# Three attentions computed with transposed scores in PSUM

## The reference

```python
x = x + tanh(g_xattn[n]) * attention_n(layernorm(x), ctx, ctx)
x = x + tanh(g_ffn[n]) * ffn_n(layernorm(x))
```

## Time and profile before

| | us |
|---|---|
| median of 3 runs | 3622.13 (3612.05 to 3623.86) |
| profiled execution | 3616.34 |
| its span | 3614.6 |
| PE / DVE / ACT / POOL busy | 2554.5 / 2132.0 / 1498.5 / 1596.1 |

### The profile page before, as it was taken

The page is one execution under the profiler, slowest core; times in us unless marked ns, Lnnn a source line. Parts: engine busy times, 40 slices in busy tenths (PEclk is TensorE's granted clock), DMA queues, the critical chain, the costliest instruction groups (busy, mean ns, idle before and its releaser), DMA issues. The chain is left out here.

```text
span 3614.6 us, 84054 instructions
## 1 busy us (share of the span) xinstructions
PE 2554.5 (71%) x30961; PEld 1981.4 (55%) x30971; DVE 2132.0 (59%) x4394; ACT 1498.5 (41%) x2492; POOL 1596.1 (44%) x2184
## 2 busy tenths in 40 slices
PE   5999999977678886233687766609956877665490
PEld 4878778764557775122465555506634665554260
DVE  3767777661166664676578788854424666677312
ACT  3555555532255553677343333202215665553120
POOL 1333433440164430775024666440017788884207
PEclk9999999988888887555688778659976766675795
DMA  4000000003300000000000000015531000000243
GB/s 143 17 18 22 23 21 21 20 8 112 99 26 22 22 19 13 1 1 1 26 10 12 23 22 23 20 61 153 161 106 32 23 25 27 27 23 13 79 128 93
DMA packets 192979, 153.50 MB, mean 42 GB/s; under 512 B 24426, under 2 KB 170461, under 8 KB 192582
## 3 DMA queue, kind: packets, MB, share of 16 engines
q1 hardware_dynamic: 176198, 116.45, 11.0%
q0 software_dynamic: 16384, 31.69, 2.9%
HBM read 97.54 MB, written 52.43 MB: 41 GB/s over the span
## 5 line engine op out<-in xcount | busy, mean ns | idle before, releaser
L979 PE MATMUL l_B<-l_val,l_prob_t 128*64 128x18 f32 x6144 | 348.6, 220 | 44.1 <-ACT l_prob_t L822 36.9
L979 PEld LDWEIGHTS l_B<-l_val,l_prob_t 128*64 128x64 f32 x6144 | 340.4, 149 | 59.3 <-issue 59.3
L903 PE MATMUL l_PT<-const_table,l_prob 128*128 128x128 f32 x1536 | 267.9, 332 | 38.0 <-ACT l_prob_t L822 28.6
L1971 PE MATMUL experts_H<-experts_xs_t,experts_w 128*128 128x512 f32 x576 | 272.1, 616 | 10.1 <-ACT experts_hid L1951 4.9
L903 PEld LDWEIGHTS l_PT<-const_table,l_prob 128*128 128x128 f32 x1536 | 237.3, 178 | 68.8 <-issue 58.0
L822 ACT COPY l_prob_t<-l_PT 128x512 f32<-128x512 f32 x384 | 209.6, 601 | 132.8 <-PE l_PT L903 132.7
L203 POOL DMA_INDIRECT l_got<-rows,l_index x192 | 220.2, 1147 | 94.7 <-POOL l_index L196 50.3
L358 POOL TENSOR_TENSOR l_products<-l_router_w,xn_all 128x1024 f32<-128x1024 f32 x100 | 236.3, 2390 | 32.3 <-DVE logits L464 32.0
L883 PE MATMUL l_A<-const_table,l_xn 128*128 128x128 f32 x192 | 59.6, 410 | 251.7 <-issue 139.1
L328 POOL DMA_INDIRECT slots<-xn_all,put x192 | 202.0, 1052 | 60.6 <-issue 49.5
L632 POOL TENSOR_TENSOR l_var_eps<-l_mv,eps 128x2 f32<-128x2 f32 x96 | 26.4, 275 | 430.4 <-DVE l_mv L775 430.3
(11 more groups left out here) (309 smaller groups left out, 6835.8 us busy)
## 6 DMA issues: line engine op xcount, KB each, us to landing
experts_w<-in_F_w SPq DMA_DIRECT2D x104, 256.0 KB, 2.9
experts_xs<-slots SPq DMA_DIRECT2D x72, 256.0 KB, 2.8
rows<-experts_y SPq DMA_DIRECT2D x72, 256.0 KB, 2.9
l_ctx_t<-in_ctx_t SPq DMA_DIRECT2D x96, 128.0 KB, 2.1
slots<-l_zeros SPq DMA_DIRECT2D x64, 96.0 KB
experts_w<-in_F_w SPq DMA_DIRECT2D x40, 128.0 KB, 2.5
slots<-l_zeros SPq DMA_DIRECT2D x8, 512.0 KB, 5.5
l_ctx_t<-in_ctx_t SPq DMA_DIRECT2D x64, 64.0 KB, 2.0
```

Of the source, the lines that this page charges most:

```text
L903: last = nc.tensor.transpose(PT[:, c % 2, P * a:P * a + P], prob[:, t.par(5), c, a // 2, 2 * (a % 2):2 * (a % 2) + 2, :].rearrange("p j k ...
L979: last = nc.tensor.matmul(B[64 * b:64 * b + 64, col:col + 18], prob_t[:, 4 * (hp // 2) + 2 * tile + hp % 2, 64 * b:64 * b + 64], val[:, t. ...
L1971: nc.tensor.matmul(H[:, c, :], w1_s[:, t.par(2), c, :], xs_t[:, t.par(2), :], start=True, stop=True).then_inc(h_filled[c], 1)
```

## The change

`attention_narrow` becomes `attention_split`, `Tail` becomes the `Router` that the wide attention already had (now shared). In L1 and L2 the scores are made twice: S as before, query rows by key columns, only to find each row's maximum; and P, key rows by query columns, in PSUM banks Z, from which the row maximum is subtracted by matmuls (the maximum is split in bf16 parts, turned by TensorE, spread on a diagonal by VectorE, and multiplied by minus ones). ScalarE takes Exp of P straight from PSUM, and the result is already the form in which TensorE multiplies it with the values, one head at a time with a column of ones for the sum. In L3 there is no maximum, and P alone is made; relu and Ln/Exp parts are kept apart and added by TensorE's accumulation. Heads are numbered so that the rows of the four heads of a group alternate row by row; the masked copies of q and k are made by four DMAs each with a row step of four into cleared buffers. In L1 and L2 one free stage lies between projection (4) and S (6), P is stage 7, values 8, stream 9; in L3 P is stage 6, values 7, stream 8. The biases of v and o enter by bf16 matmuls of three rows. `Head` loses its index copies, and gathers behind the combination of the item before.

```diff
         if t.live(out):
...
-        if t.live(s + 2) and not self.on_dve(t, s + 2):
-            pool.wait_ge(self.w_in, self.loads)
-            wait(pool, self.xn_done, n2)
-            wait(pool, self.summed, n3)
-            for tile in range(k):
-                last = nc.gpsimd.tensor_tensor(self.prod[:, tile, :, :], self.w_s[:, :, :],
-                                               g.xn[:, bass.ds(t.item(s + 2) * k + tile, 1), :].broadcast_to([P, EXPERTS, D]),
-                                               ALU.mult)
-            last.then_inc(self.multiplied, 1)
...
-            V.tensor_reduce(g.logits[:, bass.ds(t.item(s + 3) * k, k), :], self.prod[:, :, :, :], AX.X, ALU.add).then_inc(self.summed, 1)
...
+            last = nc.tensor.matmul(out[:, EXPERTS * tile:EXPERTS * tile + EXPERTS], self.xn_t[:, t.par(s + 3), tile, :], self.w_s[:, :],
+                                    start=True, stop=True)
...
-def attention_narrow(nc, g, name, gate_col, wq, bq, wk, bk, wv, bv, wo, bo, kind, mask=None, head=None, tail=None):
+def attention_split(nc, g, name, gate_col, wq, bq, wk, bk, wv, bv, wo, bo, kind, mask=None, head=None, router=None):
...
+    STAT, NORM, TURN, PROJ = 1, 2, 3, 4
+    SCORE, PROB, OUT, STREAM = (5, 6, 7, 8) if stable else (6, 7, 8, 9)
+    SLOTS_QK, SLOTS_CTX = 4, 8
+    LAST = STREAM + 1
...
+        QK = X[:, 0, :] if stable else Z[:, 0, :]
+        XV = Z[:, 1, :]
+        TOP, WO, TURNED, RANKS = X[:, 0, 0:P], X[:, 1, 0:256], X[:, 2, :], X[:, 3, :]
...
+                    slot, before = t.par(PROJ, SLOTS_QK), PROJ + SLOTS_QK
+                    if not stable:
+                        wait(sp, qk_drained, t.done(PROJ))
+                        wait(sp, s_filled, t.done(before))
+                        for j in range(4):
+                            sp.dma_start(k_m[j:P:4, slot, j, :], k_t[j:P:4, slot, :]).then_inc(k_masked[slot], 16)
+                    wait(sp, qk_drained, t.done(PROJ))
+                    wait(sp, p_filled, t.done(before))
+                    for j in range(4):
+                        sp.dma_start(q_m[j:P:4, slot, j, :], q_t[j:P:4, slot, :]).then_inc(q_masked[slot], 16)
...
+            nc.gpsimd.memset(q_m[:, :, :, :], 0.0).then_inc(cleared, 1)
+            if folded:
+                pool.wait_ge(weights_in, LOADED)
+                nc.gpsimd.tensor_scalar(hide[:, 1, :, :], mask_raw[:, 1, :, :], HIDE, -HIDE, ALU.mult, ALU.add).then_inc(hidden, 1)
...
+                V.memset(k_m[:, :, :, :], 0.0).then_inc(cleared, 1)
...
+                if t.live(SCORE) and not stable:
+                    dve.wait_ge(ready, 1)
+                    wait(dve, s_filled, n)
+                    V.tensor_reduce(top[:, :, :].rearrange("p r a -> p (r a)"), X[:, :, :].rearrange("p r (a k) -> p (r a) k", k=64),
+                                    AX.X, ALU.max).then_inc(top_done, 1)
+                    dve.wait_ge(ready, 1)
+                    wait(dve, top_done, n)
+                    wait(dve, top_filled, t.done(SCORE + 1))
+                    V.tensor_copy(split[:, :, 0, :], top[:, :, :]).then_inc(hi_done, 1)
+                    dve.wait_ge(ready, 1)
+                    wait(dve, hi_done, n)
+                    V.tensor_tensor(rest[:, :, :], top[:, :, :], split[:, :, 0, :], ALU.subtract).then_inc(rest_done, 1)
+                    dve.wait_ge(ready, 1)
+                    wait(dve, rest_done, n)
+                    V.tensor_copy(split[:, :, 1, :], rest[:, :, :]).then_inc(mid_done, 1)
+                    dve.wait_ge(ready, 1)
+                    wait(dve, mid_done, n)
+                    V.tensor_tensor(split[:, :, 2, :], rest[:, :, :], split[:, :, 1, :], ALU.subtract).then_inc(split_done, 1)
...
+                if t.live(PROB) and stable:
+                    for r in range(4):
+                        dve.wait_ge(ready, 1)
+                        wait(dve, relu_done, 4 * t.done(PROB) - 3 + r)
+                        wait(dve, o_filled, t.done(PROB + 2))
+                        V.tensor_scalar(prob_t[:, t.par(PROB), r, :], Z[:, r, :], 0.0, None, ALU.max).then_inc(plus_done, 1)
...
+                    wait(dve, top_filled, n)
+                    wait(dve, p_filled, t.done(SCORE + 2))
+                    V.tensor_tensor(top_d[:, t.par(SCORE), :, :], TOP.unsqueeze(1).broadcast_to([P, 8, P]),
+                                    g.const[:, C_AMASK:C_AMASK + 8].unsqueeze(2).broadcast_to([P, 8, P]), ALU.mult).then_inc(diag_done, 1)
...
+                n = t.done(PROB)
+                if t.live(PROB):
+                    for r in range(4):
+                        act.wait_ge(ready, 1)
+                        wait(act, p_filled, n)
+                        wait(act, o_filled, t.done(PROB + 2))
+                        if stable:
+                            nc.scalar.activation(soft[:, t.par(PROB), r, :], Z[:, r, :], ACT.Relu, scale=-1.0).then_inc(relu_done, 1)
+                        else:
+                            nc.scalar.activation(prob_t[:, t.par(PROB), r, :], Z[:, r, :], ACT.Exp).then_inc(prob_done, 1)
+                if t.live(PROJ):
+                    act.wait_ge(ready, 1)
+                    wait(act, qk_filled, t.done(PROJ))
+                    wait(act, p_filled, t.done(PROJ + SLOTS_QK))
+                    nc.scalar.activation(k_t[:, t.par(PROJ, SLOTS_QK), :], QK[:, 256:512], ACT.Identity, bias=bk_s[:, :])
+                    nc.scalar.activation(q_t[:, t.par(PROJ, SLOTS_QK), :], QK[:, 0:256], ACT.Identity, bias=bq_scaled[:, :],
+                                         scale=SCALE).then_inc(qk_drained, 1)
...
+                if turns(t):
+                    act.wait_ge(ready, 1)
+                    wait(act, turned_filled, beats(t.t, TURNED_FROM, TURNED_BEATS))
+                    if not folded and t.live(OUT):
+                        last = nc.scalar.copy(ctx_out_t[:, t.par(OUT), :], TURNED[:, 0:256])
+                    if tail and t.live(T0 + 2):
+                        last = nc.scalar.copy(tail.xn_t[:, t.par(T0 + 2), :, :], TURNED[:, 256:512].rearrange("p (k n) -> p k n", n=P))
+                    last.then_inc(turned_drained, 1)
+                if t.live(PROB) and stable:
+                    sf = soft[:, t.par(PROB), :, :].rearrange("p r n -> p (r n)")
+                    act.wait_ge(ready, 1)
+                    wait(act, relu_done, 4 * n)
+                    nc.scalar.activation(sf, sf, ACT.Ln, bias=g.const[:, C_ONES:C_ONES + 1]).then_inc(log_done, 1)
+                    act.wait_ge(ready, 1)
+                    wait(act, log_done, n)
+                    nc.scalar.activation(sf, sf, ACT.Exp, scale=-1.0).then_inc(prob_done, 1)
...
+                if t.live(PROB):
+                    slot = t.par(PROB, SLOTS_QK)
+                    pe.wait_ge(ready, 1)
+                    wait(pe, q_masked[slot], 4 * reused(t, PROB, SLOTS_QK))
+                    if stable:
+                        wait(pe, plus_done, 4 * t.done(PROB + 1))
+                    else:
+                        wait(pe, diag_done, t.done(PROB))
+                        wait(pe, qk_drained, t.done(PROJ + 1))
+                    wait(pe, xv_drained, beats(t.t - 1, TURN, XV_BEATS))
+                    wait(pe, o_drained, t.done(OUT + 1))
+                    if not stable:
+                        for tile in range(2):
+                            for b in range(2):
+                                for r in range(4):
+                                    rows = slice(32 * r, 32 * r + 32)
+                                    nc.tensor.matmul(Z[64 * b:64 * b + 64, r, 256 * tile:256 * tile + 256], minus_ones[rows, :],
+                                                     top_d[rows, t.par(PROB), 4 * tile:4 * tile + 4, 64 * b:64 * b + 64],
+                                                     start=tile == 0, stop=False)
                     for tile in range(2):
+                        for b in range(2):
+                            for r in range(4):
                                 rows = slice(32 * r, 32 * r + 32)
                                 seq = slice(128 * tile + 64 * b, 128 * tile + 64 * b + 64)
+                                last = nc.tensor.matmul(Z[64 * b:64 * b + 64, r, 256 * tile:256 * tile + 256], k_t[rows, slot, seq],
+                                                        q_m[rows, slot, :, seq], start=stable and tile == 0, stop=tile == 1 and not folded)
+                    if folded:
+                        pe.wait_ge(hidden, 2)
+                        for tile in range(2):
+                            for r in range(4):
+                                last = nc.tensor.matmul(Z[:, r, 256 * tile:256 * tile + 256], g.const_bf[:, C_IDENT:C_IDENT + P],
+                                                        hide[:, 1, 2 * t.item(PROB) + tile, :].unsqueeze(1).broadcast_to([P, 4, 64]),
+                                                        start=False, stop=tile == 1)
+                    last.then_inc(p_filled, 1)
...
```

(64 more changed lines are left out.)

976 lines of the change are left out of this document (307 added, 669 removed).

## The result

The changed kernel took 3420.84 us (median of 4 runs, 3414.72 to 3446.79), the kernel before 3618.31 us beside it: a ratio of 0.947, 95% interval 0.942 to 0.952. Forecast were 3363 us and a range of 3285 to 3510. But this holds for that comparison only. In two later comparisons, on two chips, the same program unaltered took 3706.8 and 3706.1 us, ratios of 1.022 to the kernel before (intervals 1.017 to 1.026 and 1.019 to 1.026), which itself stayed at 3624 and 3629. The chip of the first comparison is not recorded, so whether the chip or something else makes the difference is open. Where the 285 us lie is the larger part of what follows.

A forecast was written before the change was run, and what follows sets the result against it. Before the change it took TensorE to limit L1, VectorE L2, GpSimd L3. Stage gains of 57, 107 and 95 us, together 259, off the profiled 3616.3 gave 3357; the runs' median stands 5.8 above: 3363 us, range 3285 to 3510.

The forecast's parts named there:

- Which engine bounds: After the change: TensorE bounds L1 and L2; in L3 a circle of waits led by ScalarE, 14.1 us with hops.
- The router's work and VectorE's in L2: Router products and sum go (4.7 us GpSimd, 2.3 VectorE a step), the subtraction too (3.4 in L2); L2 step 14.0.
- 16 ns and 0.2 us: Values' groups: 16 ns an instruction plus 0.2 us latency, so 2.3 us for 128 and 4.3 for 256.
- rows 8: Old profile's wide attention: 4096 such 64x64 groups in 79.9 us, 19.5 ns an instruction, the source of the values' pace.
- values 4.3: L3's values' group of 256 instructions: 4.3 us in the ScalarE-led circle of 14.1 us; step 14.4.
- 10.2: L1's step in us: 9.0 at full clock, 13.6 at half; 10.2 taken, with TensorE's idle part in one piece.
- Fill and drain: Time before and after the 31 steps: L1 64 and 22 us, L2 55 and 90, L3 76 and 86.
- Rival 1: The clock stays low, 0.65 in L1 and L2: steps 11.9 and 16.3, L3 15; +143, 3506 us; chance 0.15.
- Rival 2: Values' 64x64 groups don't overlap, accumulating instructions stall: 3923 us, slower kernel from 34 ns; chance 0.09 together with Rival 3.
- Rival 3: Mask DMAs don't overlap each other: 17 us a step in L1 and L2; some 3665 us; 0.09 with Rival 2.
- The chance of "slower": Whole kernel: 0.08 that it is slower, against 0.90 faster by over 0.3% and 0.02 within.

The follow-up runs named there:

- chip C: Chip of the unaltered changed kernel's later run (3706.10 us), the one with GpSimd's indirect DMAs waiting for the values (3473.85), and that plus VectorE sum, early Ln/Exp (3300.95).
- experiments 2 and 3: Changed kernel with L3's values summed over the soft part alone, 3592.48 us; changed kernel with L3's 256 values' instructions in two passes, 3691.2 us.
- experiment 6: Changed kernel with L1's gathers left out, their rows taken as zero: L1 383.2 us for 470.7.
- 9: Changed kernel with GpSimd's gathers and scatters waiting each step for the values' group to end: 3473.85 us, ratio 0.958 to the kernel before.
- chip D: Chip of one run: changed kernel plus GpSimd's wait, VectorE sum, early Ln/Exp, and 8 filler matmuls in L1 and L2: 3220.66 us, ratio 0.890 to kernel before.

## Why the prediction was right or wrong, point by point

- **Which engine bounds.** Right: TensorE in L1 and L2, a circle led by ScalarE in L3.
- **The router's work and VectorE's in L2.** Right: GpSimd and VectorE left the path; L2's step was 14.3 for 14.0.
- **64x64 instructions at "16 ns and 0.2 us".** Right at full clock, where nothing pauses: 1.96 us for 128. The floor of 25 ns that the Trainium skill gives (TensorE: Matmul & The Clock Gate, section "Wait — 56ns, not 53.3ns?") does not hold for four 64x64 tiles in turn; rows 8 decided rightly.
- **L3's "values 4.3".** This term of the circle failed in the first comparison. I gave one figure for both clocks, though I doubled the scores' time at half clock. At half clock the instructions follow at 26 to 29 ns, and L3 has a granted clock of 0.59. The group was 7.2 us in the mean, 2.9 more; the step was 17.6, which leaves 0.3 us of hops that I can't assign: 31 x 3.2 = 99 us on the steps of L3. That the half clock does this is read from the traces; the run that was to raise the clock inside the group did not do so.
- **L1's "10.2".** 11.0: P and S ran at half clock in most steps, P's 32 matmuls 1.96 us for the 1.12 in my 1.35, under a granted clock of 0.81 where I counted on 0.84 and an idle part "in one piece". It is this piece, the wait for the diagonal, behind which they run slowly; with it filled P and S take 1.04. That this is worth 0.6 us a step in L1 rests on two chips.
- **Fill and drain.** The fills were forecast 11, 14 and 29 us too long and the drains 2, 3 and 8: 67 us of error that hid half of the 132 in the steps. That 3421 lies within 58 us of 3363 is luck to this extent.
- **Rival 1.** In the first comparison it did not occur (0.81 and 0.86 in L1 and L2). On chip C it did, 0.70 and 0.67, but together with the pauses; which part of the time each takes was not separated.
- **Rival 2, "the 64x64 groups don't overlap".** Its mechanism is refuted by experiments 2 and 3. Its threshold came out right: it put the point from which the kernel is slower at 34 ns an instruction. On chip C the 512 instructions of one step in each of the three stages take 3.49 + 4.50 + 11.14 us, 37 ns each, and the kernel is 2% slower. I had taken the pace from a stage without indirect DMAs beside it.
- **Rival 3.** It did not occur: in the traces of the first comparison and of chip C no matmul waits for a mask DMA. Its terms add up to 3677 us, not to "some 3665".
- **The chance of "slower".** 0.08 covered the three comparisons badly: in two of three it was slower, and 3706 us lies outside the range. The range had no term for differences between one comparison and another, since the kernel before shows none.

What is shown: indirect DMAs of GpSimd running beside a dense values' group make TensorE pause in it. Taken away in experiment 6 or moved in 9, the values' groups are all but free of pauses, and moving them was worth 232 us on chip C, though in L2 half of the pauses came back in P. What is not shown: by what way, nor whether GpSimd's part of an indirect DMA or its packets do it. The first pause after 40 to 50 instructions looks like a store on the way to TensorE, or one of the profile's records, that empties or fills faster than it is served. The span and clock of every timed run are on record, so none of these times is known to be one without the profiler, and this explanation stays open. The Trainium skill (Runtime: NRT & Kernel Launch, section "Instruction fetch mechanics") calls the cost of going from one 16 KiB block of instructions to the next mostly hidden; the trace of chip C agrees, as its pauses don't keep to the blocks. Why the first comparison has so much less of it (0.3 us a group in L1 for 1.1, 0.4 in L3 for 4.0) is open too.

## What to carry to other kernels

A pace read from one stage holds for what ran beside it and for its clock: before using it for a dense run of short instructions, look at the clock and at GpSimd's DMAs in the stage where it is to be used. Try indirect DMAs beside long instructions and not beside short ones, where one wait gained 232 us, and see afterwards where the pauses went: in L2 they came back in the scores. Measure a dense kernel more than once and on more than one chip before its gain is believed. And add up the errors of a forecast term by term: here a good total hid two that cancelled.

## What the hardware showed that was not expected

- One program, 3421 us in one comparison and 3706 in two later ones on two chips, where the kernel before differs by 0.4%.
- Pauses of TensorE inside dense groups while GpSimd runs indirect DMAs, from the 40th to 50th instruction on, that don't keep to the blocks in which its instructions are fetched.
- 128 f32 matmuls of 64x64 by 9 columns, with their weight loads, in 1.96 us at full clock; 26 to 29 ns each at half.
- 8 bf16 matmuls of 256 columns in a wait of 1 us (1.03 us busy) bring the 64 score matmuls behind them in L1 from medians of 1.99 and 1.57 us (chip C) to 1.05 and 1.04 (chip D); 16 such matmuls spread through L3's values did not raise the clock (0.57).
